# One 128-column matmul in place of two 64-column ones, in a four-layer graph network

## The chip, the cores and the metric

The kernel runs on one core of one Trainium2 chip. The metric is the device time of one execution in microseconds (us); lower is better. The kernel before takes 1981.38 us (median of 3 runs, 1980.59 to 1981.7). Where a text says "the profile", it means one further execution that the hardware profiler recorded.

## The reference: what is computed

There are N = 8192 nodes with 64 features each and a dense adjacency matrix `adj` of 8192 x 8192 f32 values (268 MB). Four layers run one after the other. In each, `h` is the rectified layer norm of the running `x`, and the layer's result is added to `x`:

```
h = relu(layernorm(x));  x = x + adj @ (h * keep / 0.9)                      # layer 0, dropout mask from u
h = relu(layernorm(x));  x = x + l2norm(relu([h, (adj@h + h)/deg] @ W + b))  # layer 1
h = relu(layernorm(x));  x = x + (D^-1/2 (adj + I) D^-1/2 h) @ W             # layer 2
h = relu(layernorm(x));  x = x + [h, adj@h/(deg+1)] @ W.T                    # layer 3
```

The degrees are row sums of `adj`. Nearly all of the arithmetic is the product `adj @ h`, four times, in f32.

## The kernel before

**Tiling.** `adj` is cut into 16 x 16 units of 512 x 512 values (1 MB each; 128 partitions x 2048 columns). A unit (b, g) carries the sources of row block g to the targets of row block b. A ring of 12 buffers holds units as they arrive; each diagonal unit goes to one of two `diag` buffers. SyncE issues all of these loads in one fixed order and waits, before each, until TensorE (and, where a unit is summed, VectorE) has let go of the buffer's last unit.

**A matmul.** The stationary operand is the state `h` of one tile of 128 nodes: 128 rows (contraction) x 64 columns (features). The moving operand is 512 columns of a unit. The result is 64 x 512 and goes to the lower or the upper half (partitions 0 to 63 or 64 to 127) of one of five accumulators `acc`. A 64-column matmul uses half of the array's columns, so the code always issues such matmuls in pairs, one to each half. In the records each f32 matmul stands as two LDWEIGHTS and two MATMUL.

**Sharing a load between two layers.** As soon as row g of layer L is finished its states for layer L+1 exist, so a unit in the right place of the triangle can serve both layers while it is in the ring. This gives three sweeps that load the matrix about two and a half times in place of four: sweep 1 (rows 0 to 15, downwards) serves layers 0 and 1; sweep 2 (rows 10 down to 0, after a head of four rows) layers 1 and 2; sweep 3 (rows 4 to 15, after a head) layers 2 and 3, with units of layer 3 alone in `GROUPS_AFTER` and at the end (`FINAL_ROWS`). The helper `both` (L493) handles a unit that serves two layers: for each of its 4 tiles one matmul with the state of the even part into half 0 and one with the state of the next layer into half 1, with the same moving operand. The helper `alone` (L484) handles a unit of one layer: two tiles at a time, one to each half. A `both` unit thus has 8 matmuls, an `alone` unit 4. Diagonal units (L629 to L643, L721 to L729) and the heads (`head_first`, `head_second`) pair matmuls of different banks or layers.

**What stands between the units on TensorE** (all in one program order written out by hand): `finish` (L502) multiplies a finished row by the layer's weights: 4 matmuls with 128 stationary columns and 64 moving ones into Z; `sum_degrees` (L523): 4 with 128 stationary columns and one moving; `turn_own` (L538): two transposes of 128 x 128 of the row's own states into HT; `top` (L551): two matmuls of 128 x 128 on the turned states into TOP; `add_self` (L561): 4 with 64 stationary columns (the identity moves, 128 columns).

**ScalarE** copies finished accumulator halves to `y` (`copy_y`, `copy_part`, `copy_group`), HT to SBUF (`copy_hT`), and takes square roots that VectorE asks for (`norm_root`, `degree_root`). It too has one fixed order, and a wait in it holds everything behind it. In sweep 2, for row b, its order is: wait for `z_done` of row b+1 (L418), `copy_part(b + 1)` (L419), `copy_hT(1, b)` (L420), two roots, ..., `copy_y(b)`. TensorE's order in the same row is: first unit, `finish(1, b + 1)`, `turn_own(1, b)`, second unit, `top(1, b)`, further units, `sum_degrees(2, b)` before the last one for rows 0 to 8.

**VectorE** sums units for the degrees, ends a row of a layer (normalisation, next states into `h`), and folds groups.

The states lie in two tensors `h[0]` and `h[1]` (even and odd layers); `u`, the dropout draw, is loaded into `h[1]` before that is used.

Of the kernel before, what the change touches and what calls it, by code (L numbers as in the profile page):

```python
# [131 lines left out]
def gnn_stack(nc, x_in, u_in, stream_in, w1_in, b1_in, w2_in, w3_in, x_out):  # L132
# [6 lines left out]
    with ctx:  # L139
        def sbuf(name, shape):  # L140
            return ctx.enter_context(nc.sbuf_tensor(name, shape, fp32))
# [5 lines left out]
            return ctx.enter_context(nc.semaphore(name))  # L147

        x = sbuf("x", [P, TILES * F])
        h = [sbuf(f"h{i}", [P, TILES * F]) for i in range(2)]  # L150
        u = h[1]
        ring = [sbuf(f"ring{i}", [P, UNIT]) for i in range(RING)]
        diag = [sbuf(f"diag{i}", [P, UNIT]) for i in range(2)]
        y = sbuf("y", [P, ROWS * COLS])
        row_sum = sbuf("row_sum", [P, UNIT])
        row_total = [sbuf(f"row_total{i}", [P, COLS]) for i in range(2)]
        z_sb = sbuf("z_sb", [P, FEATS])
        centred = sbuf("centred", [P, FEATS])
        squares = sbuf("squares", [P, FEATS])
        top_sb = [sbuf(f"top_sb{i}", [P, FEATS]) for i in range(5)]  # L160
        hT = [sbuf(f"hT{i}", [P, 2 * P]) for i in range(2)]
        ident = sbuf("ident", [P, P])
        ones = sbuf("ones", [P, 1])
# [39 lines left out]
        total_ready = sem("total_ready")  # L203
        deg_done = sem("deg_done")
        deg_taken = sem("deg_taken")
        hT_done = sem("hT_done")
        hT_copied = sem("hT_copied")
        top_done = sem("top_done")
# [106 lines left out]
        def _(act):  # L315
# [30 lines left out]
            def copy_part(b, bank, half):  # L346
                nc.scalar.copy(own_y(b, 1), half_of(bank, half)).then_inc(part_copied, 1)  # L347

            def copy_hT(layer, b):
                n = TOPS.index((layer, b))  # L350
                act.wait_ge(hT_done, n + 1)
                if n >= 2:
                    act.wait_ge(top_done, n - 1)
                nc.scalar.copy(hT[n % 2][:, :], HT).then_inc(hT_copied, 1)
# [10 lines left out]
            for b in range(ROWS):  # L365
                if b > 0:
                    norm_root()
                    if not DEFER[b - 1]:
                        degree_root()
                if b == LAST:  # L370
                    for r in (14, 13, 12, 11):
                        copy_hT(1, r)
                if b > 0:
                    act.wait_ge(*diag_let_go(1, b - 1))
                    act.wait_ge(z_done, rank(0, b - 1) + 1)
                    copy_part(b - 1, (b - 1) % 2, 1)
                if b == 0:
                    act.wait_ge(diag_used, 1)
                else:
                    act.wait_ge(*freed((1, b, b - 1)))  # L380
                if b < LAST:
                    copy_y_both(b, b % 2, 2 + b % 2)
                else:
                    copy_y(b, b % 2, 0)
# [3 lines left out]
            degree_root()  # L388
            act.wait_ge(*diag_let_go(1, LAST))
            copy_y_both(15, 1, 1)  # L390
            copy_hT(1, 15)
            act.wait_ge(head_done, 1)
            copy_y(14, BANK_UP[14], 0)
# [21 lines left out]
            for b in range(LAST - 1 - HEAD, -1, -1):  # L415
                if b < LAST - 1 - HEAD:

                    act.wait_ge(z_done, rank(1, b + 1) + 1)  # L418
                    copy_part(b + 1, BANK_UP[b + 1], 1)  # L419
                copy_hT(1, b)  # L420
                norm_root()
                norm_root()
                if DEFER[b]:
                    degree_root()
                act.wait_ge(*freed((2, b, b + 1)))
                copy_y(b, BANK_UP[b], 0)

            act.wait_ge(z_done, rank(1, 0) + 1)
            copy_part(0, BANK_UP[0], 1)  # L430
            norm_root()
            norm_root()
            act.wait_ge(head_done, 4 + 2)
# [16 lines left out]
            copy_part(3, BANK_DOWN[3], 1)  # L450
            for b in range(HEAD, ROWS):
                for r in TOPS_LATE[b]:
                    copy_hT(3, r)
                if b > HEAD:
                    act.wait_ge(*diag_let_go(3, b - 1))
                    copy_part(b - 1, BANK_DOWN[b - 1], 1)
                act.wait_ge(*freed((3, b, b - 1)))
                copy_y(b, BANK_DOWN[b], 0)
                norm_root()
                for quad, r in GROUPS_AFTER[b]:  # L460
                    if opens_row(quad, r):
                        copy_group(quad, r)

            copy_hT(3, 14)
            copy_hT(3, 15)
            act.wait_ge(*diag_let_go(3, LAST))
            copy_y_both(LAST, BANK_DOWN[LAST], BANK_DOWN[LAST])
# [4 lines left out]
        @block.tensor  # L473
        def _(pe):
            def mm(bank, half, layer, J, moving, start, stop):
                return nc.tensor.matmul(half_of(bank, half), h[layer % 2][:, J * F:(J + 1) * F], moving,  # L476
                                        start=start, stop=stop)

            def await_unit(key, *layers):
                pe.wait_ge(*loaded(key))  # L480
# [9 lines left out]
                              first and k == 0, last_high and k == 2)  # L490
                done.then_inc(unit_freed, 1)

            def both(key, layer, bank, first, first_next, last, last_next):  # L493

                for k in range(TPR):
                    J = key[2] * TPR + k
                    mm(bank, 0, layer, J, source_tile(slot(key), k), first and k == 0, last and k == TPR - 1)
                    done = mm(bank, 1, layer + 1, J, source_tile(slot(key), k),
                              first_next and k == 0, last_next and k == TPR - 1)
                done.then_inc(unit_freed, 1)  # L500

            def finish(layer, b):  # L502
# [35 lines left out]
            def turn_own(layer, b):  # L538
                nonlocal turned
                n = TOPS.index((layer, b))  # L540
                pe.wait_ge(*state(layer, b))
                if n >= 1:
                    pe.wait_ge(hT_copied, n)
                pe.wait_ge(deg_taken, summed)
                turned = n + 1
                for k in range(2):
                    at = b * FEATS + k * P
                    mm_t = nc.tensor.transpose(HT[:, k * P:(k + 1) * P], h[layer % 2][:, at:at + P], ident[:, :])  # L548
                mm_t.then_inc(hT_done, 1)

            def top(layer, b):  # L551
# [9 lines left out]
            def add_self(bank, half, b):  # L561

                pe.wait_ge(*state(2, b))
                for t in range(TPR):
                    at = (b * TPR + t) * F
                    nc.tensor.matmul(half_of(bank, half)[:, t * P:(t + 1) * P], h[0][:, at:at + F], ident[:, :],  # L566
                                     start=False, stop=False)

            def head_first(phase, step, behind=None):
# [34 lines left out]
            for b in range(ROWS):  # L604
# [10 lines left out]
                    pe.wait_ge(part_copied, PARTS.index((1, b - 2)) + 1)  # L615
                for g in range(b - 1):
                    await_unit((1, b, g), 0, 1)
                    both((1, b, g), 0, low, b == LAST and g == 0, g == 0, False, False)
                    if b == LAST and g == 0:
                        finish(0, b - 1)  # L620
                        sum_degrees(1, b - 1)
                    if b == LAST and 3 <= g <= 10:
                        if g % 2:
                            turn_own(1, 14 - (g - 3) // 2)
                        else:
                            top(1, 14 - (g - 3) // 2)
                        if g == 3:
                            pe.wait_ge(weights_loaded, 11 * 16)
# [6 lines left out]
                else:  # L635
# [6 lines left out]
                    used.then_inc(diag_used, 1)  # L642
                    done.then_inc(diag_freed, 1)  # L643
                    await_unit((1, b, b - 1), 0, 1)
                    both((1, b, b - 1), 0, low, False, b == 1, True, False)

            pe.wait_ge(part_copied, PARTS.index((1, 14)) + 1)
# [18 lines left out]
            for b in range(LAST - 1 - HEAD, -1, -1):  # L667
# [3 lines left out]
                for g in range(LAST, b, -1):  # L671
                    if g == b + 1 and DEFER[b]:
                        sum_degrees(2, b)
                    await_unit((2, b, g), 1, 2)
                    both((2, b, g), 1, BANK_UP[b], g == LAST, g == LAST, g == b + 1, g == b + 1)
                    if g == LAST:
                        if b < LAST - 1 - HEAD:
                            finish(1, b + 1)
# [21 lines left out]
            for b in range(HEAD, ROWS):  # L700
# [8 lines left out]
                tops = TOPS_LATE[b]  # L709
                for i, g in enumerate(range(b - 1)):  # L710
                    await_unit((3, b, g), 2, 3)
                    both((3, b, g), 2, bank, i == 0, i == 0, False, False)
                    if unfinished:
                        finish(2, unfinished.pop())
                    if i == 0:
# [12 lines left out]
                if b > HEAD:  # L728
                    done.then_inc(diag_freed, 1)  # L729
                await_unit((3, b, b - 1), 2, 3)  # L730
                both((3, b, b - 1), 2, bank, False, False, True, False)
                unfinished.append(b)
                for quad, r in GROUPS_AFTER[b]:
                    n = GROUPS.index((quad, r))
# [45 lines left out]
        def _(dve):  # L780
# [35 lines left out]
            def prologue(q):  # L816
# [4 lines left out]
                dve.wait_ge(xu_loaded[q], 32)  # L821
                layer_norm(x[:, part], cen, sq, n)
                chain(nc.vector.tensor_scalar(inverse[:, 0:n], inverse[:, 0:n], 1.0 / (1.0 - P_DROP), None, ALU.mult))
                chain(nc.vector.scalar_tensor_tensor(out=by_tile(h[0][:, part]), in0=by_tile(cen), scalar=0.0,
                                                     in1=spread(inverse[:, 0:n]), op0=ALU.max, op1=ALU.mult))
                nc.vector.scalar_tensor_tensor(out=h[0][:, part], in0=u[:, part], scalar=P_DROP, in1=h[0][:, part],
                                               op0=ALU.is_ge, op1=ALU.mult).then_inc(h_ready, 1)

            def take_z(layer, b):
# [13 lines left out]
            def next_states(layer, b, scale=None):  # L843
                xs, v = own(x, b), inverse[:, 0:TPR]
                layer_norm(xs, centred[:, :], squares[:, :], TPR)
                if scale is not None:
                    chain(nc.vector.tensor_tensor(v, v, scale, ALU.mult))
                nc.vector.scalar_tensor_tensor(out=by_tile(own(h[(layer + 1) % 2], b)), in0=by_tile(centred[:, :]),  # L848
                                               scalar=0.0, in1=spread(v), op0=ALU.max,
                                               op1=ALU.mult).then_inc(h_ready, 1)  # L850
                dve.wait_ge(*state(layer + 1, b))
# [195 lines left out]
```

## Time and profile before

| | |
|---|---|
| median of 3 runs | 1981.38 us |
| profiled execution, whole | 1981.27 us |
| its span, first to last instruction | 1979.4 us |
| TensorE busy | 1927.1 us (97%) |
| VectorE busy | 881.2 us (45%) |
| ScalarE busy | 102.8 us (5%) |
| granted TensorE clock, mean | 0.999 |
| read from memory | 667 MB, 338 GB/s over the span |

A row of a busy table gives an engine's busy time, its share and the number of instructions. PE is TensorE's matmul side, PEld its weight loads, DVE VectorE, ACT ScalarE, POOL GpSimd, SPq SyncE's queue of load issues. The chain of waits is the work that ended last, followed back from release to release: what is on it sets the time, the rest is hidden.

### The profile page before, as it was taken

Reading aid. Unit: us, or ns where it says so; the run is one execution under the profiler, and the core shown is the slowest. Engines: PE = TensorE matmul, PEld = TensorE weight load, DVE = VectorE, ACT = ScalarE, POOL = GpSimd, SP = SyncE. Lnnn points to the kernel's source line nnn. Section 1 sums busy time; section 2 is a strip of 40 time slices with the busy share of each in tenths; the row PEclk is TensorE's granted clock in tenths of the full one; section 3 lists DMA queues with packets and bytes.
Section 4 is the critical chain, followed back from the end, with each engine's and each line's share of the span. In section 5 each row is a group of like instructions: output and inputs, shape, how many; then the busy total and the mean of one; then the engine's idle time right before and its main releaser. Section 6 shows DMA issues by size and latency. Waiting matters only on the chain.

```text
span 1979.4 us, 22145 instructions
## 1 busy us (share of the span) xinstructions
PE 1927.1 (97%) x9224; PEld 704.6 (36%) x9224; DVE 881.2 (45%) x1098; ACT 102.8 (5%) x243; POOL 11.6 (1%) x29
## 2 busy tenths in 40 slices
PE   5899999999999999999999999999999999999998
PEld 1233333333333333333333333433333333333343
DVE  6365767788878865435455465211111000100221
ACT  0000000000000001100000000100000000000000
POOL 0000000000000000000000000000000000000000
PEclk9999999999999999999999999999999999999999
DMA  9999999998888773867767777586999889989898
GB/s 390 421 421 421 421 422 420 421 402 340 340 329 329 311 268 123 332 263 296 278 237 299 290 281 275 223 371 253 370 365 356 338 291 418 362 350 412 347 422 343
DMA packets 93968, 670.63 MB, mean 339 GB/s; under 512 B 11440, under 2 KB 11440, under 8 KB 12976
## 3 DMA queue, kind: packets, MB, share of 16 engines
q1 hardware_dynamic: 92160, 666.94, 83.6%
q0 software_dynamic: 768, 2.10, 0.3%
q8 instruction: 75, 1.23, 0.2%
q10 hardware_dynamic: 944, 0.20, 0.1%
q14 instruction: 21, 0.17, 0.0%
HBM read 667.09 MB, written 2.10 MB: 338 GB/s over the span
## 4 chain that ended last, share of the span: by engine, by line
PE 89%; DMA 9%; DVE 2%; issue 0%; SPq 0%; ACT 0%; POOL 0%; DVEq 0%
PE acc L476 83%; DMA ring<-stream_in 6%; DMA diag<-stream_in 3%; PE Z L517 3%; PE TOP L557 1%; PE HT_DEG L534 1%; PE acc L566 1%; PE HT_DEG L548 1%; DVE h L848 0%; ACT y L340 0%; DVE row_sum L892 0%; DVE row_sum L886 0%; DVE squares L810 0%; DVE z_sb L840 0%; DVE centred L808 0%
## 5 line engine op out<-in xcount | busy, mean ns | idle before, releaser
L476 PE MATMUL acc<-ring,h 128*64 128x512 f32 x7744 | 1710.4, 595 | 44.5 <-DMA ring<-stream_in 37.2
L476 PEld LDWEIGHTS acc<-ring,h 128*64 128x64 f32 x7744 | 550.4, 137 | 1101.1 <-issue 1032.5
L886 DVE TENSOR_TENSOR row_sum<-row_sum,ring 128x2048 f32<-128x2048 f32 x190 | 435.6, 2292 | 13.9 <-DMA ring<-stream_in 8.5
L840 DVE TENSOR_TENSOR z_sb<-Z,deg_rsqrt 128x256 f32<-128x256 f32 x16 | 6.8, 425 | 382.4 <-PE Z L517 382.3
L476 PE MATMUL acc<-diag,h 128*64 128x512 f32 x448 | 104.4, 598 | 2.6 <-DMA diag<-stream_in 2.6
L886 DVE TENSOR_TENSOR row_sum<-ring 128x2048 f32<-128x2048 f32 x25 | 57.3, 2293 | 71.0 <-DMA ring<-stream_in 69.1
L517 PEld LDWEIGHTS Z<-below,y 128*128 128x128 f32 x512 | 61.9, 191 | 51.2 <-issue 27.6
L347 ACT COPY y<-acc 64x512 f32<-64x512 f32 x45 | 26.2, 582 | 916.2 <-PE acc L476 875.2
L517 PE MATMUL Z<-below,y 128*128 128x64 f32 x512 | 70.5, 281 | 0.9 <-DVE y L951 0.9
L476 PEld LDWEIGHTS acc<-diag,h 128*64 128x64 f32 x448 | 33.7, 137 | 67.1 <-issue 62.6
L942 DVE TENSOR_TENSOR x<-TOP,x 128x256 f32<-128x256 f32 x16 | 6.8, 425 | 112.4 <-PE TOP L557 112.4
L955 DVE TENSOR_TENSOR y<-acc,y 128x512 f32<-128x512 f32 x21 | 14.5, 692 | 83.9 <-PE acc L476 83.9
L840 DVE TENSOR_TENSOR z_sb<-Z,deg_clipped 128x256 f32<-128x256 f32 x16 | 6.8, 425 | 89.5 <-PE Z L517 89.4
L920 DVE TENSOR_TENSOR degree<-HT_DEG,degree 128x4 f32<-128x4 f32 x9 | 1.5, 163 | 97.7 <-PE HT_DEG L534 97.7
L855 DVE TENSOR_TENSOR x<-Z,x 128x256 f32<-128x256 f32 x16 | 6.8, 424 | 73.5 <-PE Z L517 73.5
L892 DVE TENSOR_TENSOR row_sum<-row_sum,diag 128x2048 f32<-128x2048 f32 x16 | 36.7, 2292 | 6.1 <-DMA diag<-stream_in 5.9
L896 DVE TENSOR_TENSOR row_sum<-row_sum 128x1024 f32<-128x1024 f32 x25 | 30.6, 1225 | 0.9
L807 DVE TENSOR_REDUCE mean<-x 128x4 f32<-128x256 f32 (+1 forms) x52 | 25.0, 481 | 7.5 <-DMA h<-u_in 5.8
L534 PEld LDWEIGHTS HT_DEG<-ones,row_total 128*128 128x128 f32 x200 | 24.3, 192 | 7.8 <-issue 7.3
L331 ACT ACTIVATE rooted<-to_root 128x4 f32<-128x4 f32 (+1 forms) x68 | 14.1, 207 | 232.0 <-DVE to_root L797 213.7
L557 PEld LDWEIGHTS TOP<-above,hT 128*128 128x128 f32 x128 | 16.7, 190 | 26.0 <-issue 25.2
L534 PE MATMUL HT_DEG<-ones,row_total 128*128 128x1 f32 x200 | 25.6, 249 | 0.3 <-DVE row_total L900 0.3
(61 smaller groups left out, 402.7 us busy)
## 6 DMA issues: line engine op xcount, KB each, us to landing
ring<-stream_in SPq DMA_DIRECT2D x604, 1024.0 KB, 10.2
diag<-stream_in SPq DMA_DIRECT2D x28, 1024.0 KB, 11.2
x<-x_in SPq DMA_DIRECT2D x4, 512.0 KB, 6.6
h<-u_in SPq DMA_DIRECT2D x4, 512.0 KB, 7.5
x_out<-x POOLq DMA_DIRECT2D x16, 128.0 KB, 5.5
below<-w_in ACTq DMA_DIRECT2D x6, 16.0 KB, 7.1
above<-w_in ACTq DMA_DIRECT2D x4, 16.0 KB, 6.3
bias<-b_in ACTq DMA_DIRECT2D x1, 32.0 KB, 12.0
```

The lines of the kernel that those rows point to most:

```text
L347: nc.scalar.copy(own_y(b, 1), half_of(bank, half)).then_inc(part_copied, 1)
L476: return nc.tensor.matmul(half_of(bank, half), h[layer % 2][:, J * F:(J + 1) * F], moving, start=start, stop=stop)
L517: mm_z = nc.tensor.matmul(Z[:, t * F:(t + 1) * F], own_y(b)[:, t * P:(t + 1) * P], below[:, layer, :], start=True, stop=True)
L534: mm_d = nc.tensor.matmul(DEG[:, t:t + 1], row_total[n % 2][:, t * P:(t + 1) * P], ones[:, :], start=True, stop=True)
L548: mm_t = nc.tensor.transpose(HT[:, k * P:(k + 1) * P], h[layer % 2][:, at:at + P], ident[:, :])
L557: mm_t = nc.tensor.matmul(TOP[:, k * 2 * F:(k + 1) * 2 * F], hT[n % 2][:, k * P:(k + 1) * P], above[:, layer, :], start=True, stop=True)
L566: nc.tensor.matmul(half_of(bank, half)[:, t * P:(t + 1) * P], h[0][:, at:at + F], ident[:, :], start=False, stop=False)
L807: chain(nc.vector.tensor_reduce(m, by_tile(xs), X, ALU.add))
L886: nc.vector.tensor_tensor(row_sum[:, :], before, slot(key)[:, :], ALU.add).then_inc(unit_summed, 1 if count > 1 else 2)
L892: chain(nc.vector.tensor_tensor(row_sum[:, :], row_sum[:, :], diag_slot(1, b)[:, :], ALU.add))
L896: chain(nc.vector.tensor_tensor(row_sum[:, 0:2 * COLS], row_sum[:, 0:2 * COLS], row_sum[:, 2 * COLS:4 * COLS], ALU.add))
L955: nc.vector.tensor_tensor(own_y(r), acc[bank][:, :], own_y(r), ALU.add).then_inc(group_folded, 1)
```

## The change

The states of both layers of one tile now lie side by side in one tensor `states`, so that 128 neighbouring columns are the stationary operand for both halves of an accumulator. `both` issues one such matmul for a tile in place of two, wherever both halves start and stop their accumulation together; where they do not (the first tile of a row's first unit in sweep 1, except in the last row, and the last tile of the unit next to the diagonal in sweeps 1 and 3), it issues the pair as before. In sweep 2 the two layers change halves. The four tiles of one row's state are no longer neighbours in memory, so a new ScalarE step `pack` copies them together before `turn_own`, which now waits for that copy and no longer for the state itself. `u` moves into a part of `y`.

```diff
-        h = [sbuf(f"h{i}", [P, TILES * F]) for i in range(2)]
-        u = h[1]
+        states = sbuf("states", [P, TILES * 2 * F])
+        h = [states[:, :].rearrange("p (t l f) -> p l t f", l=2, f=F)[:, i] for i in range(2)]
+        u = y[:, 2 * FEATS:2 * FEATS + TILES * F]
...
+            def pack(layer, b):
+
+                n = TOPS.index((layer, b))
+                act.wait_ge(*state(layer, b))
+                if n >= 2:
+                    act.wait_ge(hT_done, n - 1)
+                nc.scalar.copy(by_tile(packed[n % 2][:, :]),
+                               h[layer % 2][:, b * TPR:(b + 1) * TPR]).then_inc(packed_ready, 1)
...
                     for r in (14, 13, 12, 11):
+                        pack(1, r)
                         copy_hT(1, r)
...
             copy_y_both(15, 1, 1)
+            pack(1, 15)
             copy_hT(1, 15)
...
                     act.wait_ge(z_done, rank(1, b + 1) + 1)
-                    copy_part(b + 1, BANK_UP[b + 1], 1)
+                    copy_part(b + 1, BANK_UP[b + 1], 0)
+                pack(1, b)
                 copy_hT(1, b)
...
                 for r in TOPS_LATE[b]:
+                    pack(3, r)
                     copy_hT(3, r)
...
-            def both(key, layer, bank, first, first_next, last, last_next):
+            def both(key, bank, first, first_odd, last, last_odd):
 
                 for k in range(TPR):
                     J = key[2] * TPR + k
-                    mm(bank, 0, layer, J, source_tile(slot(key), k), first and k == 0, last and k == TPR - 1)
-                    done = mm(bank, 1, layer + 1, J, source_tile(slot(key), k),
-                              first_next and k == 0, last_next and k == TPR - 1)
+                    moving = source_tile(slot(key), k)
+                    starts, starts_odd = first and k == 0, first_odd and k == 0
+                    stops, stops_odd = last and k == TPR - 1, last_odd and k == TPR - 1
+                    if (starts, stops) == (starts_odd, stops_odd):
+                        done = nc.tensor.matmul(acc[bank][:, :], states[:, J * 2 * F:(J + 1) * 2 * F], moving,
+                                                start=starts, stop=stops)
+                    else:
+                        mm(bank, 0, 0, J, moving, starts, stops)
+                        done = mm(bank, 1, 1, J, moving, starts_odd, stops_odd)
                 done.then_inc(unit_freed, 1)
...
             def turn_own(layer, b):
...
-                pe.wait_ge(*state(layer, b))
+                pe.wait_ge(packed_ready, n + 1)
...
-                    mm_t = nc.tensor.transpose(HT[:, k * P:(k + 1) * P], h[layer % 2][:, at:at + P], ident[:, :])
+                    mm_t = nc.tensor.transpose(HT[:, columns], packed[n % 2][:, columns], ident[:, :])
```

## Rows read from the trace of the kernel before

**Rows 1.** The page's busy times, and its costliest TensorE group.

```profile
PE 1927.1 (97%) x9224; PEld 704.6 (36%) x9224; DVE 881.2 (45%) x1098; ACT 102.8 (5%) x243; POOL 11.6 (1%) x29
L476 PE MATMUL acc<-ring,h 128*64 128x512 f32 x7744 | 1710.4, 595 | 44.5 <-DMA ring<-stream_in 37.2
```

**Rows 2.** Chain of waits in sweep 2: start us, length us, what it was.

```profile
1118.98 1.04 PE Z L517 x8
1120.02 0.23 PE HT_DEG L548 x2
1120.24 3.58 PE acc L476 x16
1123.82 0.64 PE TOP L557 x4
1124.47 37.92 PE acc L476 x176
1162.38 0.98 PE HT_DEG L534 x8
```

**Rows 3.** Timeline of one `top`: start, stretch; its line: ns min/median/max.

```profile
1123.75 0.52 PEld L557 LDWEIGHTS TOP<-above,hT 128*128 128x128 f32 x4 [0.81 <-issue]
1123.75 0.71 PE L557 MATMUL TOP<-above,hT 128*128 128x128 f32 x4
...
L557 PE MATMUL TOP<-above,hT x128: 275/275/377, 719.4 to 1869.3; 128*128 128x128 f32 x128
```

**Rows 4.** Timeline: `add_self` and `turn_own` at the start of row 8 of sweep 3.

```profile
1384.60 1.09 PE L566 MATMUL acc<-ident,h 128*64 128x128 f32 x8
1385.61 0.20 PEld L548 LDWEIGHTS HT_DEG<-ident,h 128*128 128x128 f32 x2 [0.17 <-issue]
1387.72 0.21 ACT L331 ACTIVATE rooted<-to_root 128x4 f32<-128x4 f32 x1 [6.89 <-DVE to_root L797]
```

**Rows 5.** Busy time by stretch: engines' us (instructions), granted clock, DMA share, GB/s.

```profile
176.00:203.00 27.00, 25.93 (x126) 9.69 (x122) 14.78 (x17) 1.95 (x4) 0.00 (x0) 1.00 1.01 421
808.00:1218.00 410.00, 410.00 (x1974) 148.89 (x1969) 207.24 (x310) 22.98 (x63) 0.00 (x0) 1.00 0.75 296
1420.00:1845.00 425.00, 425.00 (x2024) 150.44 (x2022) 34.75 (x81) 14.48 (x33) 0.00 (x0) 1.00 0.92 361
1845.00:1850.00 5.00, 5.00 (x25) 1.49 (x21) 0.00 (x0) 1.07 (x2) 0.00 (x0) 1.00 0.32 79
```

**Rows 6.** Chain of waits: the `finish` in rows 5, 6 and 7 of sweep 1.

```profile
224.72 1.03 PE Z L517 x8
...
265.64 1.04 PE Z L517 x8
...
307.58 1.03 PE Z L517 x8
```

**Rows 7.** Timeline: `turn_own(1, b)` and ScalarE in one row of sweep 2.

```profile
1119.74 0.26 PEld L548 LDWEIGHTS HT_DEG<-ident,h 128*128 128x128 f32 x2
1120.05 0.58 ACT L347 COPY y<-acc 64x512 f32<-64x512 f32 x1 [3.88 <-PE Z L517]
1120.66 0.37 ACT L354 COPY hT<-HT_DEG 128x256 f32<-128x256 f32 x1
```

**Rows 8.** Timeline after the last diagonal unit of sweep 1, and the head's end.

```profile
775.92 0.20 PEld L548 LDWEIGHTS HT_DEG<-ident,h 128*128 128x128 f32 x2 [0.81 <-issue]
776.64 0.58 ACT L344 COPY y<-acc 64x512 f32<-64x512 f32 x1
806.96 5.37 PE L476 MATMUL acc<-ring,h 128*64 128x512 f32 x24 [0.89 <-DVE h L848]
```

**Rows 9.** Timeline at the start of row 12 of sweep 3: ScalarE and `turn_own`.

```profile
1579.83 0.56 ACT L360 COPY y<-acc 64x512 f32<-64x512 f32 x1
1581.04 0.20 PEld L548 LDWEIGHTS HT_DEG<-ident,h 128*128 128x128 f32 x2 [0.17 <-issue]
```

**Rows 10.** Chain of waits at the end of the span.

```profile
1946.35 25.11 DMA ring<-stream_in
```

More of the change, by code:

```diff
@@ L160, in gnn_stack @@
         top_sb = [sbuf(f"top_sb{i}", [P, FEATS]) for i in range(5)]
+        packed = [sbuf(f"packed{i}", [P, FEATS]) for i in range(2)]
         hT = [sbuf(f"hT{i}", [P, 2 * P]) for i in range(2)]
@@ L205, in gnn_stack @@
         deg_taken = sem("deg_taken")
+        packed_ready = sem("packed_ready")
         hT_done = sem("hT_done")
@@ L425, in _ @@
                 act.wait_ge(*freed((2, b, b + 1)))
-                copy_y(b, BANK_UP[b], 0)
+                copy_y(b, BANK_UP[b], 1)
             act.wait_ge(z_done, rank(1, 0) + 1)
-            copy_part(0, BANK_UP[0], 1)
+            copy_part(0, BANK_UP[0], 0)
             norm_root()
@@ L462, in _ @@
                         copy_group(quad, r)
+            pack(3, 14)
             copy_hT(3, 14)
+            pack(3, 15)
             copy_hT(3, 15)
@@ L475, in mm @@
             def mm(bank, half, layer, J, moving, start, stop):
-                return nc.tensor.matmul(half_of(bank, half), h[layer % 2][:, J * F:(J + 1) * F], moving,
-                                        start=start, stop=stop)
+                return nc.tensor.matmul(half_of(bank, half), h[layer % 2][:, J], moving, start=start, stop=stop)
             def await_unit(key, *layers):
@@ L546, in turn_own @@
                 for k in range(2):
-                    at = b * FEATS + k * P
-                    mm_t = nc.tensor.transpose(HT[:, k * P:(k + 1) * P], h[layer % 2][:, at:at + P], ident[:, :])
+                    columns = slice(k * P, (k + 1) * P)
+                    mm_t = nc.tensor.transpose(HT[:, columns], packed[n % 2][:, columns], ident[:, :])
                 mm_t.then_inc(hT_done, 1)
@@ L564, in add_self @@
                 for t in range(TPR):
-                    at = (b * TPR + t) * F
-                    nc.tensor.matmul(half_of(bank, half)[:, t * P:(t + 1) * P], h[0][:, at:at + F], ident[:, :],
+                    nc.tensor.matmul(half_of(bank, half)[:, t * P:(t + 1) * P], h[0][:, b * TPR + t], ident[:, :],
                                      start=False, stop=False)
@@ L617, in _ @@
                     await_unit((1, b, g), 0, 1)
-                    both((1, b, g), 0, low, b == LAST and g == 0, g == 0, False, False)
+                    both((1, b, g), low, b == LAST and g == 0, g == 0, False, False)
                     if b == LAST and g == 0:
@@ L644, in _ @@
                     await_unit((1, b, b - 1), 0, 1)
-                    both((1, b, b - 1), 0, low, False, b == 1, True, False)
+                    both((1, b, b - 1), low, False, b == 1, True, False)
             pe.wait_ge(part_copied, PARTS.index((1, 14)) + 1)
@@ L674, in _ @@
                     await_unit((2, b, g), 1, 2)
-                    both((2, b, g), 1, BANK_UP[b], g == LAST, g == LAST, g == b + 1, g == b + 1)
+                    both((2, b, g), BANK_UP[b], g == LAST, g == LAST, g == b + 1, g == b + 1)
                     if g == LAST:
@@ L711, in _ @@
                     await_unit((3, b, g), 2, 3)
-                    both((3, b, g), 2, bank, i == 0, i == 0, False, False)
+                    both((3, b, g), bank, i == 0, i == 0, False, False)
                     if unfinished:
@@ L730, in _ @@
                 await_unit((3, b, b - 1), 2, 3)
-                both((3, b, b - 1), 2, bank, False, False, True, False)
+                both((3, b, b - 1), bank, False, False, True, False)
                 unfinished.append(b)
@@ L823, in prologue @@
                 chain(nc.vector.tensor_scalar(inverse[:, 0:n], inverse[:, 0:n], 1.0 / (1.0 - P_DROP), None, ALU.mult))
-                chain(nc.vector.scalar_tensor_tensor(out=by_tile(h[0][:, part]), in0=by_tile(cen), scalar=0.0,
+                fresh = h[0][:, q * n:(q + 1) * n]
+                chain(nc.vector.scalar_tensor_tensor(out=fresh, in0=by_tile(cen), scalar=0.0,
                                                      in1=spread(inverse[:, 0:n]), op0=ALU.max, op1=ALU.mult))
-                nc.vector.scalar_tensor_tensor(out=h[0][:, part], in0=u[:, part], scalar=P_DROP, in1=h[0][:, part],
+                nc.vector.scalar_tensor_tensor(out=fresh, in0=by_tile(u[:, part]), scalar=P_DROP, in1=fresh,
                                                op0=ALU.is_ge, op1=ALU.mult).then_inc(h_ready, 1)
@@ L847, in next_states @@
                     chain(nc.vector.tensor_tensor(v, v, scale, ALU.mult))
-                nc.vector.scalar_tensor_tensor(out=by_tile(own(h[(layer + 1) % 2], b)), in0=by_tile(centred[:, :]),
+                nc.vector.scalar_tensor_tensor(out=h[(layer + 1) % 2][:, b * TPR:(b + 1) * TPR], in0=by_tile(centred[:, :]),
                                                scalar=0.0, in1=spread(v), op0=ALU.max,
```

## The prediction

> **What bounds the kernel now.** I read the page's busy times first: TensorE is busy for 97% of the span, and nearly all of it in the 64-column matmuls of L476 [rows 1]. Busy is not bound, so the chain of waits came next. In sweeps 2 and 3 it is TensorE from end to end [rows 2]; the busy table by stretch agrees, with TensorE at 410.00 of 410 us and the transfers at 0.75 of their capacity in sweep 2, and 425.00 of 425 against 0.92 in sweep 3 [rows 5]. Two places differ. Early in sweep 1 transfers run at 421 GB/s and 1.01 of their capacity while TensorE idles [rows 5]. A row of that sweep needs 16 MB, that is 16.8 / 0.421 = 39.9 us of transfer; from one `finish` to the next the chain has 40.9 us for row 5 and 41.9 for row 6 [rows 6], and each later row has one `alone` unit less and one `both` unit more. I take rows 1 to 5 as bound by transfers and rows 6 to 15 by TensorE. The end is bound by transfers again: the chain holds one wait of 25.11 us for loads [rows 10]. But from 1845 to 1850 us the DMA share is only 0.32 [rows 5]: the ring is full there, so the last loads are counted from TensorE's time at 1850 us, and whatever TensorE loses or gains before is passed on whole. What changes after 1850 us is hidden.
>
> **The steady stream: nothing.** An f32 pair is four MATMUL records. From the stretches of 176 and of 16 records, (37.92 - 3.58) / 160 = 0.2146 us a record, so a pair of tiles' worth takes 0.858 us: each half of the array streams one record in 0.429 us, both at once [rows 2]. After the change the same tile is two records of 128 columns. Is one of them also 0.429 us? No row has 128 stationary and 512 moving columns. The nearest is `top`: four records in 0.71 us; the first lasts 0.377, being 0.10 late for its weights, the others 0.275, so they come every (0.71 - 0.377) / 3 = 0.111 us for 128 moving columns [rows 3]. `add_self`, 64 stationary and also 128 moving, has eight in 1.09 us, and with the same last duration 0.27 and 0.05 of entry that is again 0.11 each [rows 4]. Wide matmuls will be 4 x 344 units (120 in sweep 1, 110 in sweep 2, 114 in sweep 3) less the 41 tiles that stay pairs: 1335, or 2670 records. The ends are -2670 x 0.0025 = -7 us and +2670 x 0.017 = +45 us; the value nearest to both rows is 0.
>
> The Trainium skill, "TensorE: Matmul & The Clock Gate", Part 3 (What overlaps and what doesn't), has a rule that speaks against this: a weight load overlaps a matmul in flight only when the row groups differ, and full-height operands never differ. By it every wide record would show its weight load. The rows of `top` speak the other way: load and matmul both come every 0.11 us.
>
> **Changes of width: -2 us.** Going from 64 to 128 columns and back costs time. An `acc` stretch of 16 records takes 3.58 us where 16 x 0.2146 = 3.43, so 0.15 of entry; `top` takes 0.64 where four records at 0.1115 are 0.45 [rows 2, 3]. One excursion from narrow matmuls to `top` and back costs 0.15 + 0.64 - 0.45 = 0.34 us over its streaming. In the same way `finish` with `turn_own` has 0.15 + 1.04 + 0.23 - 10 x 0.1115 = 0.30, and `sum_degrees` 0.15 + 0.98 - 8 x 0.1115 = 0.24 [rows 2]; a turn or a `finish` alone I price at 0.30 too. Between two wide units this goes away. In sweep 1's last row: 4 tops, 4 turns and one `finish` with degrees; in sweep 2: 11 tops, 10 times `finish` and turn, one turn, 9 degrees; in sweep 3: 14 tops, 2 turns, one `finish`. That is 29 at 0.34, 18 at 0.30 (7 turns, 10 pairs, one `finish`) and 10 at 0.24 (degrees): 17.6 us saved.
> New changes of width arise where wide units meet narrow ones. Rows 2 to 14 of sweep 1 go wide after the first tile of g = 0, narrow for the diagonal, wide for three tiles and narrow for the last: 2 round trips each; row 1 has 1, row 15 has 2, sweep 2 as a whole 1. Each of the 12 rows of sweep 3 has 2 (the one at `add_self` takes the place of the one that `turn_own` had). Of these the 9 in rows 1 to 5 of sweep 1 lie under transfers; 18 + 2 + 1 + 24 = 45 are exposed. I price them like `top`, which loads 128 weights on entry and 64 on return: 45 x 0.34 = 15.3 us. If one costs only what `sum_degrees` shows it is 10.8. Net -2.3 us, between -7 and 0.
>
> The same skill's "TensorEngine Tiling (Array Packing)", Key Properties, says that changing the tiling mode, not just the tile, drains the engine. By that rule these 45 are real; if the excess of 0.24 to 0.34 us belonged instead to the other target bank or the short moving operand, both sides of this term would be 0.
>
> **The new copy: +17.8 us.** `pack` takes 128 x 256 values; ScalarE's copy of that size is 0.37 us [rows 7]. ScalarE is busy 5% [rows 1], so 32 copies (12 us) cost it nothing; the question is what each makes `turn_own` wait for.
> In sweep 2, rows 9 to 0, it stands in ScalarE's order behind a wait for `z_done` and `copy_part`. TensorE does `finish(1, b + 1)` and goes straight on to the transposes, at 1119.74, while ScalarE only starts the part's copy at 1120.05, because it waited for that very `finish` [rows 7]. After the change: part copied until 1120.63, pack 1120.66 to 1121.03, TensorE 0.04 later at 1121.07. That is 1.33 us idle, with all units of the row queued behind. Nothing covers it: TensorE is the chain, the transfers have room, so a full ring gives nothing back. 10 x 1.33 = 13.3 us. Bounds: if the copy from SBUF were free 0.96 each, if it took the 0.58 of a copy of 512 columns 1.54: 9.6 to 15.4.
> Row 15's turn: the transposes began at 775.92, right behind the diagonal; now they come after two copies (the second ends at 777.22), `pack` and 0.04, at 777.66: +1.74 us [rows 8]. Behind it wait `top`, `finish(1, 15)` and the whole chain of VectorE through the head, which TensorE still awaits at 806.96 [rows 8]; so it is passed on whole.
> Row 8 of sweep 3: row 7 has no group behind it, so `finish(2, 7)` comes just before `turn_own(3, 6)`, and ScalarE's order has the root of that row (1387.72 to 1387.93) ahead of `pack`. Transposes at 1385.61 become 1387.95 + 0.37 + 0.04 = 1388.36: +2.75 us [rows 4]. In row 12 (and 7) one unit and the group's copy lie between: the copy ends at 1580.39, pack at 1580.80, the transposes came at 1581.04 [rows 9]: free by 0.2 us. The other rows have more room. Turns at 14 and 15 of the last layer come after 1850 us and are hidden.
> Next states are written in chunks of 64 before as after; `u` elsewhere moves nothing on a queue, and the start is bound by loads: 0.
>
> **Sum.** Against the profiled execution, 1981.27 us (span 1979.4 and 1.87 around it; 0.11 below the median of the runs): 0 - 2.3 + 13.3 + 1.74 + 2.75 = +15.5, so 1996.8 us, 0.8% slower. A change of 0.2%, 4 us, is about what a measurement tells from none.
>
> **Rivals.**
> (a) *Changes of width cost nothing between wide-moving matmuls.* A saving at `top` is measured; a price where one 512-column matmul follows another of the other width is not. If it is 0, the sum is 15.5 - 15.3 = +0.2, 1981.5: no change. For it: no row has such a neighbour. Against it: entering 128 columns shows 0.10 us for weights and the rest is idle whatever comes before. 5%.
> (b) *Faster.* As (a), and each wide record takes 0.427 in place of 0.429, since one record and not two has the fixed part, -7 us: 1974.8. It decides from (4 + 0.2) / 2670 = 0.0016 us a record on if (a) holds; alone it would need (15.5 + 4) / 2670 = 0.0073, and over 1024 cycles only 0.0025 is there to take. Against: both halves already run side by side at 0.429. 4%.
> (c) *The weight load of 128 columns is not covered*, as that page's rule has it. A wide record then takes 0.11 more: +2670 x 0.11 = +294, some 2290 us. Against: [rows 3]. 2%.
> (d) *Wide records a little slower*, 0.4315, a seventh of the way to the upper end: +2670 x 0.0023 = +6, 2003 us. Nothing in the rows rules it out. 10%.
> (e) *The change doesn't do what it says*: the flags let too few tiles through. By the code 1335 of 1376 pass, so 1%.
>
> **How the numbers follow.** Forecast 78%: 1996.8, with the copy's bounds (-3.7, +2.1) and the net of widths (-5, +2.3) 1989 to 2001. Rival (d) reaches to 2006. Range 1989 to 2005, for 8 in 10 and a little more. Faster by over 0.2% comes from (b), 4%, and a part of (a), 1%: 0.05; within 0.2% the rest of (a): 0.04; slower 0.91.
>
> **What would show it.** 2670 MATMUL records with 128 columns and 2852 with 64 (8192 - 4 x 1335), the wide ones every 0.429 us. `top` between wide units 0.45 us with no entry of 0.15. In sweep 2 ten idle times of about 1.3 us on TensorE before L548's line, ended by ScalarE's new copy; one of 1.7 near 776 and one of 2.7 in sweep 3. The stretch of sweep 2 (410 us) longer by 13.3 - 9 = 4 us, since 11 tops, 11 turns and 9 degrees save some 9 there. I am wrong if that stretch is shorter, or if wide records are not at 0.429.

## The result and the profile after

The changed kernel takes 1998.18 us (median of 4 runs, 1997.03 to 1998.73) beside 1981.15 us for the kernel before (median of 4 runs): a ratio of 1.0085, 95% interval 1.0072 to 1.0097. It is slower by 17.0 us; the prediction was 1996.8 us, 15.5 slower. Two executions of the experiments below, one of e3_pairs (3421.13 us, mean granted clock 0.556) and one of e5_early_pairs (8151.84 us, 0.236), are left out of every median and ratio; no other run has a mean clock under 0.991.

The page of the profile after: the span, the engines' busy us, then groups (line, engine, operation, shape, count, busy us, mean ns, idle before).

```profile
span 1996.8 us, 16867 instructions
...
PE 1930.5 (97%) x6554; PEld 815.1 (41%) x6554; DVE 881.2 (44%) x1098; ACT 114.0 (6%) x275; POOL 11.6 (1%) x29
...
L519 PE MATMUL acc<-ring,states 128*128 128x512 f32 x2670 | 1173.8, 595 | 0.0
...
L495 PE MATMUL acc<-ring,states 128*64 128x512 f32 x2404 | 550.6, 602 | 42.7 <-DMA ring<-stream_in 34.8
...
L495 PE MATMUL acc<-diag,states 128*64 128x512 f32 x448 | 104.4, 598 | 2.2 <-DMA diag<-stream_in 2.2
...
L572 PE MATMUL HT_DEG<-ident,packed 128*128 128x128 f32 x64 | 13.6, 294 | 15.3 <-ACT packed L359 15.3
```

TensorE has 2670 fewer matmul records than before (6554 against 9224 [rows 1]) and is busy for 1930.5 us, not less than the 1927.1 of before. 2670 records are wide and 2404 + 448 = 2852 narrow, as counted. New is the last line: 15.3 us in which TensorE stood idle until ScalarE's `pack`.

The chain of waits in sweep 2, the stretch that answers to [rows 2]:

```profile
1127.91 0.85 PE Z L541 x8
1128.77 0.02 issue
1128.79 0.02 ACT y L351
...
1129.39 0.41 ACT packed L359
1129.81 0.04 issue
1129.85 0.44 PE HT_DEG L572 x2
1130.29 3.44 PE acc L519 x8
1133.72 0.45 PE TOP L581 x4
1134.17 37.77 PE acc L519 x88
1171.93 0.79 PE HT_DEG L558 x8
```

Three things are to be seen. The wide stream: 37.77 / 88 = 0.4292 us a record, and 176 narrow records took 37.92 with their entry [rows 2]. The excursion to `top`: 0.45 us where it was 0.64, and the unit ahead of it 3.44 where it was 3.58 [rows 2]. And ScalarE now stands on the chain between `finish` and the transposes. The timeline of the same place answers to [rows 7]:

```profile
1128.79 0.58 ACT L351 COPY y<-acc 64x512 f32<-64x512 f32 x1 [3.69 <-PE Z L541]
...
1129.39 0.41 ACT L359 COPY packed<-states 128x256 f32<-128x256 f32 x1
...
1129.85 0.44 PE L572 MATMUL HT_DEG<-ident,packed 128*128 128x128 f32 x2 [1.10 <-ACT packed L359]
```

TensorE's own gap reads 1.10 us, but the units behind it come 1.3 us later: here the first matmul of the next unit starts 2.37 us after the first of `finish` (1127.75 to 1130.12), and without the wait (run e2_early below) 1.07 us after it (1115.25 to 1116.32). Part of the difference lies outside the gap, because without the wait the transposes start before the last record of `finish` has ended (1116.09 against 1116.25).

In sweep 1 one row on the chain now falls into pieces (from one `finish` to the next, 51.81 us in the kernel before; L519 is the wide form, L495 the narrow one):

```profile
545.23 1.03 PE Z L541 x8
...
547.11 4.44 PE acc L495 x20
551.55 37.11 PE acc L519 x86
588.66 3.58 PE acc L495 x16
592.24 2.77 PE acc L519 x6
595.01 2.73 PE acc L495 x12
597.74 1.04 PE Z L541 x8
```

Wide twice, narrow twice, 597.74 - 545.23 = 52.51 us: 0.70 more, for two round trips of width.

### The profile page after: what moved, and what is told of

It reads as the page before. It is cut to its first block, busy times and chain, and to the rows that moved or that the text cites. A ratio compares the mean times of both kernels' runs of the same rounds, so it can differ in the third digit from the quotient of the medians.

```text
span 1996.8 us, 16867 instructions
## 1 busy us (share of the span) xinstructions
PE 1930.5 (97%) x6554; PEld 815.1 (41%) x6554; DVE 881.2 (44%) x1098; ACT 114.0 (6%) x275; POOL 11.6 (1%) x29
## 4 chain that ended last, share of the span: by engine, by line
PE 88%; DMA 8%; DVE 2%; issue 1%; ACT 1%; SPq 0%; POOL 0%; ACTq 0%; DVEq 0%
PE acc L519 58%; PE acc L495 25%; DMA ring<-stream_in 6%; DMA diag<-stream_in 3%; PE Z L541 3%; PE HT_DEG L558 1%; PE TOP L581 1%; PE acc L589 1%; PE HT_DEG L572 1%; ACT packed L359 0%; DVE centred L831 0%; DVE z_sb L864 0%; DVE states L872 0%; DVE squares L833 0%; DVE mean L830 0%
## 5 line engine op out<-in xcount | busy, mean ns | idle before, releaser
L519 PE MATMUL acc<-ring,states 128*128 128x512 f32 x2670 | 1173.8, 595 | 0.0
L519 PEld LDWEIGHTS acc<-ring,states 128*128 128x128 f32 x2670 | 498.3, 190 | 624.0 <-issue 624.0
L495 PE MATMUL acc<-ring,states 128*64 128x512 f32 x2404 | 550.6, 602 | 42.7 <-DMA ring<-stream_in 34.8
L495 PEld LDWEIGHTS acc<-ring,states 128*64 128x64 f32 x2404 | 165.5, 137 | 377.8 <-issue 318.2
L495 PE MATMUL acc<-diag,states 128*64 128x512 f32 x448 | 104.4, 598 | 2.2 <-DMA diag<-stream_in 2.2
L351 ACT COPY y<-acc 64x512 f32<-64x512 f32 x45 | 26.1, 581 | 915.8 <-PE acc L495 876.6
L495 PEld LDWEIGHTS acc<-diag,states 128*64 128x64 f32 x448 | 30.2, 136 | 72.2 <-issue 68.1
L572 PE MATMUL HT_DEG<-ident,packed 128*128 128x128 f32 x64 | 13.6, 294 | 15.3 <-ACT packed L359 15.3
```

The source lines that it names most:

```text
L519: done = nc.tensor.matmul(acc[bank][:, :], states[:, J * 2 * F:(J + 1) * 2 * F], moving, start=starts, stop=stops)
L572: mm_t = nc.tensor.transpose(HT[:, columns], packed[n % 2][:, columns], ident[:, :])
```

## The experiments

All were timed beside the kernel before on the same chip. The first four shared runs of the kernel before at 1981.16 us (median), the last four, on another chip, at 1981.22. Where a text gives the length of a row, it is the time from one `finish` to the next on the profile's chain of waits.

**e1_row8: pack for row 8 of sweep 3 ahead of the root.**

```diff
                 for r in TOPS_LATE[b]:
-                    pack(3, r)
+                    if b != 8:
+                        pack(3, r)
...
                 copy_y(b, BANK_DOWN[b], 0)
+                if b == 7:
+                    pack(3, 6)
                 norm_root()
```

> The changed kernel, with one copy moved: pack for row 6 is issued before the root of row 7's end in sweep 3, so turn_own at the start of row 8 finds it ready. Theory: the changed kernel lost 2.56 us of idle TensorE there plus 1.70 us because the granted clock was 0.5 for 3.4 us behind that idle time; both go, 1998.2 - 4.3 = 1993.9 us, and no stretch at 0.5 is left in sweep 3. Rival (the clock fell for another reason, such as the wide matmuls): only the idle time goes, 1995.6 us, and the 0.5 stays somewhere in sweep 3.

Measured: 1992.84 us, ratio 1.006 (1.0046 to 1.0074): 5.3 us off the changed kernel, where 4.3 was expected. The two profiled executions (1998.56 and 1992.28) differ by 6.3 us: 4.36 lie between the `finish` before row 8 and the one behind it, as the theory has it; the rest is 0.6 in the first rows and 1.3 in the last loads, with no cause in the edit. What the changed kernel did at row 8, busy us by stretch (PE, PEld, DVE, ACT, POOL, then granted clock, DMA share, GB/s):

```profile
1395.00:1398.00 3.00, 0.41 (x5) 0.17 (x3) 2.52 (x8) 0.50 (x2) 0.00 (x0) 1.00 1.00 423
1399.00:1402.00 3.00, 3.00 (x5) 1.14 (x4) 0.00 (x0) 0.00 (x0) 0.00 (x0) 0.50 1.00 421
```

TensorE idles for 2.59 us in the first stretch; in the second it is busy all the time, at a granted clock of 0.50, the lower of its two levels (1.2 GHz), and its wide records take longer. The timeline has the eight of that unit in one stretch:

```profile
1397.94 0.44 PE L572 MATMUL HT_DEG<-ident,packed 128*128 128x128 f32 x2 [2.59 <-ACT packed L359]
1398.21 5.30 PE L519 MATMUL acc<-ring,states 128*128 128x512 f32 x8
```

At full clock they take 7 x 0.429 + 0.59 = 3.60 us (seven spacings and the length of the last record): 1.7 us lost. With the copy moved, no stretch at 0.50 is left in sweep 3.

**e2_early: all packs ahead of what they stood behind.** Row 8 as above, and:

```diff
+            pack(1, 15)
             act.wait_ge(*diag_let_go(1, LAST))
             copy_y_both(15, 1, 1)
-            pack(1, 15)
...
+                pack(1, b)
                 if b < LAST - 1 - HEAD:

                     act.wait_ge(z_done, rank(1, b + 1) + 1)
                     copy_part(b + 1, BANK_UP[b + 1], 0)
-                pack(1, b)
```

> The changed kernel with pack moved ahead of what it stood behind in all three places (row 8 as in the run before; row 15's pack before the two copies of y; pack(1, b) before the wait for z_done in sweep 2). Theory: the waits were the whole loss. 10 x 1.26 in sweep 2, 1.78 at row 15, 4.26 at row 8: 1998.2 - 18.6 = 1979.6 us, 1 to 3 us under the kernel before, which is the net of the changes of width (-2.3). Rival (wide matmuls or the new layout cost something by themselves): it stays above 1983 us.

Measured: 1978.51 us, ratio 0.9986 (0.9977 to 0.9994), 1.1 us under the 1979.6 expected and clear of the rival's 1983. The chain in the same row of sweep 2:

```profile
1115.42 0.84 PE Z L544 x8
1116.25 0.22 PE HT_DEG L575 x2
1116.48 3.44 PE acc L522 x8
```

ScalarE is gone from it. Against e1 this is 14.3 us for eleven waits; by the length of the rows they are ten of 1.31 and one of 1.8, 14.9 in all. The place of three lines on an engine that is busy 6% made the whole slowdown.

**e3_pairs: every tile a pair, packs as in the change.**

```diff
-                    if (starts, stops) == (starts_odd, stops_odd):
+                    if (starts, stops) == (starts_odd, stops_odd) and False:
```

> The changed kernel with every tile as a pair of 64-column matmuls, the new layout and pack left as they are. Theory: the changes of width saved (17.6) and cost (15.3) nearly the same, so 1998.2 + 2.3 = 2000.5 us. Rival (a) of the prediction, changes between 512-column matmuls are free: the savings alone would go, 1998.2 + 17.6 = 2015.8 us.

Measured: 1998.95 us (three runs, 1998.57 to 2001.27), ratio 1.0093 (1.0077 to 1.0108). That excludes the 2015.8 of free changes; it is 0.8 us above the changed kernel, where 2.3 was expected. The profile gives the rest: at the `finish` ahead of the last loads it is 0.60 us behind the changed kernel's, although it did not lose the 1.7 us of clock behind the idle time at row 8 (last section). 0.60 + 1.70 = 2.3, the term as predicted; row by row it is 0.70 faster in sweep 1, 2.3 slower in its last row, 0.93 slower in each row of sweep 2 that has degrees and 0.35 faster in a full row of sweep 3.

**e4_last_narrow: the unit next to the diagonal as pairs.**

```diff
-                    if (starts, stops) == (starts_odd, stops_odd):
+                    if (starts, stops) == (starts_odd, stops_odd) and not (key[0] in (1, 3) and key[2] == key[1] - 1):
```

> The changed kernel with the unit next to the diagonal as four pairs in sweeps 1 and 3, so that rows go narrow at the diagonal and stay so: one round trip of width less in each. Theory: 9 + 1 exposed in sweep 1 and 12 in sweep 3, 22 x 0.34 = 7.5 us less, 1990.7 us. Rival (a), changes free between 512-column matmuls: 1998.2 us, no difference.

Measured: 1989.29 us, ratio 1.0039 (1.0027 to 1.0052), 8.9 us less. Each of the rows named is 0.35 us shorter. In the two profiled executions (1998.56 and 1987.47) the difference is 11.1 us: 7.7 in the 22 rows, 1.7 because the same idle time at row 8 was not followed by a fall of the clock, and the rest in the first rows and the last loads. How much of the 1.4 us that the medians show beyond the 7.5 expected is the clock, is not shown.

```profile
1389.00:1392.00 3.00, 0.77 (x8) 0.53 (x5) 2.57 (x7) 0.19 (x2) 0.00 (x0) 1.00 1.01 429
1393.00:1396.00 3.00, 3.00 (x8) 1.33 (x7) 0.00 (x0) 0.21 (x1) 0.00 (x0) 1.00 1.01 429
```

Its runs lie 3.6 us apart (1987.47 to 1991.07), those of the kernel before 1.8; a fall that comes in some executions would do that. Its two shortest runs have a mean granted clock of 1.000, the other three of 0.996 to 0.999; this fits, but the mean takes in the start and the end of the span too, and only one execution was profiled.

**e5_early_pairs: e2_early with every tile a pair**, so layout, copies and the place of `u` alone.

```diff
-                    if (starts, stops) == (starts_odd, stops_odd):
+                    if (starts, stops) == (starts_odd, stops_odd) and False:
```

> Pack moved ahead as in e2_early, and every tile as a pair of 64-column matmuls: what is left of the change is the layout side by side, the copies and the place of u. Theory: these cost nothing, 1981.2 us, the time of the kernel before. Rival (the strided states or 32 more copies on ScalarE cost something): above 1983 us.

Measured: 1981.01 us (eleven runs), ratio 1.0 (0.9992 to 1.0009). All of this costs nothing, the 32 copies on ScalarE among it: from row 7 of sweep 1 to the end of sweep 3 every row of its profile is as long as in the kernel before, to 0.02 us.

**e6_alternate: in sweep 2 tiles 0 and 2 wide, 1 and 3 as pairs.**

```diff
-                    if (starts, stops) == (starts_odd, stops_odd):
+                    if (starts, stops) == (starts_odd, stops_odd) and (key[0] != 2 or k % 2 == 0):
```

> The changed kernel with tiles 0 and 2 of each unit of sweep 2 wide and tiles 1 and 3 as pairs: two round trips of width per unit, 110 units, 219 more than the changed kernel has. It prices a round trip between 512-column matmuls. Theory: 0.34 us each as at top, +75, 2073 us. At the price seen at sum_degrees, 0.24: 2051 us. Rival (a), changes between 512-column matmuls are free: 1998 us.

Measured: 2074.58 us, ratio 1.0471 (1.0457 to 1.0484). (2074.58 - 1998.18) / 219 = 0.349 us a round trip. TensorE's timeline (each stretch is one tile):

```profile
1000.22 1.08 PE L495 MATMUL acc<-ring,states 128*64 128x512 f32 x4
1001.23 1.13 PE L519 MATMUL acc<-ring,states 128*128 128x512 f32 x2
1002.28 1.08 PE L495 MATMUL acc<-ring,states 128*64 128x512 f32 x4
```

2.06 us for two tiles that take 1.72 in a stream of one width. Rival (a) falls: the price holds between two matmuls of 512 moving columns into one bank, so neither another target bank nor a short moving operand is needed for it.

**e7_where_it_saves: packs early, wide only between two 128-column operations.** The packs as in e2_early, and:

```diff
+            def wide(key):
+                phase, b, g = key
+                if phase == 1:
+                    return b == LAST and 4 <= g <= 10
+                if phase == 3:
+                    tops = len(TOPS_LATE[b])
+                    return 1 <= g <= 2 * tops - 1
+                return True
...
-                    if (starts, stops) == (starts_odd, stops_odd):
+                    if (starts, stops) == (starts_odd, stops_odd) and wide(key):
```

> Pack moved ahead as in e2_early, and wide matmuls only where a 128-column operation stands on both sides of them: all of sweep 2, units 4 to 10 of the last row of sweep 1, unit 1 (1 to 3 in rows 5 and 6) of each row of sweep 3. Theory: nearly all savings and next to no new changes of width. Sweep 2: 11 x 0.34 + 11 x 0.30 + 9 x 0.24 - 0.34 = 8.9; last row of sweep 1: 4 x 0.34 + 4 x 0.30 - 0.34 = 2.2; sweep 3: 12 x 0.30 + 2 x 0.64 = 4.9. 1981.2 - 16.0 = 1965.2 us. Rival (the savings are not what e2_early gained by): 1978 us or more.

Measured: 1964.03 us, ratio 0.9913 (0.99 to 0.9926): 17.2 us faster than the kernel before and 34 faster than the change. Its page has 1064 wide records, two fifths of those of the change:

```profile
L531 PE MATMUL acc<-ring,states 128*128 128x512 f32 x1064 | 466.6, 593 | 0.0
```

Against the kernel before it gains 2.29 us in the last row of sweep 1, 0.93 in each row of sweep 2 that has degrees (0.34 + 0.30 + 0.24 was the estimate), and 0.35 in a full row of sweep 3.

**e8_longer_idle: three more copies ahead of pack in sweep 2**, for rows 9 to 0.

```diff
+                for _ in range(more):
+                    nonlocal copies
+                    copies += 1
+                    nc.scalar.copy(by_tile(packed[n % 2][:, :]),
+                                   h[layer % 2][:, b * TPR:(b + 1) * TPR]).then_inc(idle_step, 1)
+                    act.wait_ge(idle_step, copies)
...
-                pack(1, b)
+                pack(1, b, 3 if b < LAST - 1 - HEAD else 0)
```

> The changed kernel with three more copies ahead of pack in rows 9 to 0 of sweep 2 (the same copy again, to no use), so that each of these ten waits is 1.35 us longer and about as long as the one at row 8 of sweep 3, behind which the profile of the changed kernel had the clock at 0.5 for 3.4 us. Theory 1 (an idle time of this length brings the clock down each time): 1998.2 + 13.5 + 10 x 1.7 = 2028.7 us and ten stretches at 0.5. Theory 2 (it does so only at times): 2012 to 2025 us, with fewer stretches than idle times. Rival (the fall at row 8 had another cause): 2011.7 us and no stretch at 0.5 in sweep 2.

Measured: 2026.1 us, ratio 1.0227 (1.0214 to 1.024). Its profile has ten gaps of 2.40 to 2.41 us on TensorE in sweep 2. Behind the first no stretch at 0.5 follows, behind each of the other nine one does, as here (a gap ending at 865.9):

```profile
863.00:866.00 3.00, 0.59 (x6) 0.46 (x5) 1.87 (x5) 2.19 (x5) 0.00 (x0) 1.00 0.11 46
867.00:870.50 3.50, 3.50 (x6) 1.49 (x5) 2.96 (x10) 0.20 (x1) 0.00 (x0) 0.53 0.00 0
```

The idle time brings the fall, in most cases and not in all, as Theory 2 has it, but nearly as often as Theory 1 says: 2026.1 is 1.1 us above the range given for Theory 2 and 2.6 under Theory 1. The sum with the falls counted is 1998.2 + 13.1 + 9 x 1.7 = 2026.6. A row with a fall is 3.38 us longer than in the kernel before, where the change had 0.38: 1.3 of it is the longer gap, 1.7 the clock.

## Why the prediction was right

**Stream, 0 us: right.** 0.4292 us a record in both widths, and the 128-column load is covered, as `top` had shown. The rows of before left -7 to +45 us open here; that the value is 0 within this was a choice, and to that extent luck. The rule of the Trainium skill that was weighed there ("TensorE: Matmul & The Clock Gate", Part 3) does not hold for these operands: 88 wide records, each with its own load, whose record is 0.19 us long, took 37.77 us, 0.4292 a record.

**Changes of width, -2.3 us: right.** e5 against e2 isolates it: 1981.0 - 1978.5 = 2.5. The price of 0.34 taken from `top` is 0.349 in e6. The split was off in a small place: row 6 of sweep 1 lost 0.27, not 0.68, since it still waited in part for loads before: it took 41.94 us there and takes 41.51 with every tile a pair in e3, 42.21 in the change. (The lower end of the range, by the prediction's own terms, is 1996.8 - 3.7 - 5 = 1988.1 and not 1989.)

**The waits for pack, +13.3 and +1.74: right.** 14.3 us between e1 and e2, 14.9 by the length of the rows, where 15.0 was forecast. Two small errors cancel in it: the copy took 0.41 us, not the 0.37 of ScalarE's copy of HT, and the sum counted each wait from the weight load of the transposes (1119.74), while their matmul began 0.11 us later. The stretch of sweep 2 that was to be 4 us longer is 4.2 longer: between the same two `finish` it takes 395.21 us (838.14 to 1233.35) where it took 391.01 (832.49 to 1223.50).

**Row 8, +2.75 us: the term that was mis-sized.** The idle time was right (2.59 on TensorE's line). What was not in the sum is that the clock fell behind it: the profile after lost 1.7 us more, 4.3 in all. e1, in which idle time and fall are both gone, and e8, in which nine of ten longer waits have a fall behind them, show that it came from the idle time. The prediction took idle time at its length; for the waits of 1.1 and 1.7 us that is right, no fall followed one.

**After 1850 us, hidden: right in kind.** What the kernel lost before 1850 us was passed on whole. But in the profiled execution the wait for the last loads is 26.27 us, against 25.11 [rows 10]:

```profile
1962.55 26.27 DMA ring<-stream_in
```

That 1.2 us has no cause in the change that the runs show: e1, e2, e4 and e5 have 25.0 to 25.2, e7 25.4, e6 25.7, e3 26.1 and e8 26.3. Its cause stays open. It is within the 1.7 us between the runs of the changed kernel. In the profiled execution the clock and this are 2.9 us over the forecast, and the waits and widths some 1 us under it; the median came out 1.4 above. So the forecast came this close partly because errors of both signs met.

## What to carry to other kernels

Two matmuls side by side, each on half the columns, already fill the array: a tile takes 0.858 us as a pair and as one full-width matmul. What the width decides is its changes; count them at every neighbour, keep the wide form where its neighbours are wide (1964 us in place of 1981) and don't mix it into a narrow stream (0.35 us each time). And where an edit adds a copy that another engine must wait for, read that engine's program order, not its load: ScalarE was busy for 6%, and where three lines stood in its order cost 19.7 us (1998.2 against 1978.5); the same copies placed earlier cost nothing.

## What the runs showed of the hardware that was not expected

TensorE's granted clock fell from 1.0 to 0.5 (2.4 to 1.2 GHz) 0.5 to 1.3 us after it had taken up work again behind a gap of 2.4 us or more: after 9 of 10 gaps of 2.4 us in e8 and one of 2.84 there, after the gap of 2.59 us in the profiles of the change and of e6, but not in those of e3 and e4. Wide matmuls do not bring it by themselves: e4 has them behind the same gap and no fall, and in the first 70 us it fell in the kernel before, which has none. Whether they make it likelier is not shown; the only such gap with pairs behind it is that of e3. Behind fifty gaps of 1.10 us and six of 1.71 in the profiles of the change and of e1, e3, e4, e6 and e8 it did not fall. The other places are the time after TensorE's last matmul, where it costs nothing, and the first 70 us, where waits for loads follow each other closely: there five of the ten profiles have one stretch at 0.5, that of before behind a gap of 2.09 us, the others behind two gaps of 1.2 to 1.9 us, which e1, e3 and e4 have too without a fall. In sweeps 2 and 3 each fall cost 1.7 us, so a gap of 2.6 us can cost 4.3. What decides in which execution it comes was not tried.

The Trainium skill's "TensorEngine Tiling (Array Packing)", Key Properties, says that a change of tiling mode drains the engine. The trace agrees that each change costs time, and e6 gives the number: 0.35 us for there and back in f32, weights included. That the loss is a drain and not something else at the change, no run here shows.
